# Attention block of a per-image kernel: projections split and moved, sums regrouped, four banks for the last exponent tiles, output projection in another order

## What is computed

```python
x = conv_attention(x) * gamma + x           # 32 channels, small
t = tokens(x)                               # 1024 x 256
h = layer_norm(t)
q1, k1, q2, k2, v = h@Q1.T, h@K1.T+b1, h@Q2.T, h@K2.T+b2, h@V.T     # 8 heads of 32
a1 = softmax(q1 @ k1.T / sqrt(32)); a2 = softmax(q2 @ k2.T / sqrt(32))
o = (a1 - lam * a2) @ v                     # per head
y = group_norm(o, 4 groups over all positions) @ out_w.T + out_b
t = t + y
t = t + shared_ffn(layer_norm(t)) + top2_of_8_experts(layer_norm(t))
```

## Time and profile before

| | us |
|---|---|
| median of 3 runs | 6351.29 (6344.42 to 6355.15) |
| the profiled execution's own time | 6343.51 |
| its span, first to last instruction | 6341.7 |
| TensorE busy in it | 5935.0 (94%) |
| VectorE busy | 4638.3 (73%) |
| ScalarE busy | 3218.9 (51%) |
| GpSimd busy | 3091.0 (49%) |

### The profile page before, as it was taken

One profiled execution on the slowest core, in us unless ns is written; L12 is line 12 of the kernel. 1 busy time (PEld: TensorE's weight loads), 2 busy tenths in 40 slices (PEclk: granted clock), 3 DMA queues, 4 the chain that ended last, 5 costly groups with the idle time before them and its releaser, 6 DMA issues.

```text
span 6341.7 us, 127068 instructions
## 1 busy us (share of the span) xinstructions
PE 5935.0 (94%) x41264; PEld 3784.5 (60%) x41264; DVE 4638.3 (73%) x6519; ACT 3218.9 (51%) x5724; POOL 3091.0 (49%) x1382
## 2 busy tenths in 40 slices
PE   6999999999999999999999999999999999999999
PEld 4565565655656556565565756656565565655656
DVE  5767777677776777767777677777777767677776
ACT  4545545455554545535455354554545545455454
POOL 3716537175370744707447073471735617256272
PEclk9999999999999999999999999999999999999999
DMA  2212222222222222222122221222212222121221
GB/s 74 56 49 54 58 51 51 59 49 56 53 46 59 54 55 50 46 58 55 54 52 45 62 54 53 51 48 57 55 51 53 47 60 56 46 57 44 65 56 44
DMA packets 148338, 339.05 MB, mean 53 GB/s; under 512 B 38224, under 2 KB 60880, under 8 KB 139216
## 3 DMA queue, kind: packets, MB, share of 16 engines
q1 hardware_dynamic: 147664, 330.38, 21.4%
HBM read 90.49 MB, written 17.30 MB: 17 GB/s over the span
## 4 chain that ended last, share of the span: by engine, by line
PE 70%; DVE 14%; issue 7%; ACT 4%; DMA 3%; SPq 1%; DVEq 0%; ACTq 0%
PE psum L997 16%; PE psum L1214 13%; PE psum L1145 12%; PE psum L1166 11%; DVE minus_max L742 6%; PE psum L1273 6%; PE psum L1173 4%; DVE recip_sum L763 2%; PE psum L1242 2%; DVE stage L737 2%; DMA stack<-stage 2%; PE psum L1193 1%; PE psum L1046 1%; ACT probs L497 1%; PE psum L1151 1%
## 5 line engine op out<-in xcount | busy, mean ns | idle before, releaser
L354 POOL TENSOR_TENSOR prob_sums<-probs 128x1024 f32<-128x1024 f32 x752 | 1794.4, 2386 | 3055.0 <-ACT probs L497 2629.8
L497 ACT ACTIVATE probs<-psum 128x512 f32<-128x512 f32 x4096 | 2222.6, 595 | 1428.0 <-PE psum L1214 1417.6
L742 DVE TENSOR_REDUCE minus_max<-psum 128x1 f32<-128x1024 f32 x2048 | 2417.6, 1207 | 415.7 <-PE psum L1145 410.8
L1214 PE MATMUL psum<-stack 98*128 98x512 f32 x4096 | 1451.3, 432 | 43.4 <-ACT probs L497 43.4
L1145 PE MATMUL psum<-stack 96*128 96x512 f32 x4096 | 1261.0, 414 | 129.8 <-DVE stage L737 70.7
L354 POOL TENSOR_TENSOR prob_sums<-prob_sums,probs 128x1024 f32<-128x1024 f32 x512 | 1220.2, 2383 | 72.1 <-ACT probs L497 35.7
L1166 PE MATMUL psum<-probs,v_tokens 128*32 128x256 f32 x16384 | 1111.8, 388 | 0.0
L1214 PEld LDWEIGHTS psum<-stack 98*128 98x128 f32 x4096 | 713.6, 191 | 581.0 <-ACT probs L497 447.4
L1145 PEld LDWEIGHTS psum<-stack 96*128 96x128 f32 x4096 | 725.3, 192 | 472.7 <-DVE minus_max L742 129.1
L997 PE MATMUL psum<-act_hi,w_hi 128*128 128x512 f32 x1730 | 702.3, 406 | 45.3 <-issue 26.7
L1166 PEld LDWEIGHTS psum<-probs,v_tokens 128*32 128x32 f32 x16384 | 429.0, 109 | 474.6 <-issue 297.9
(11 more groups left out here) (154 smaller groups left out, 4618.9 us busy)
## 6 DMA issues: line engine op xcount, KB each, us to landing
stack<-stage SPq DMA_DIRECT2D x1024, 128.0 KB, 3.1
stack<-stage SPq DMA_DIRECT2D x256, 256.0 KB, 3.0
prob_sums<-combine_rows_dram SPq DMA_DIRECT2D x128, 256.0 KB, 3.8
stage<-combine_rows_dram SPq DMA_DIRECT2D x128, 256.0 KB, 4.1
x_tile<-x_dram SPq DMA_DIRECT2D x17, 1024.0 KB, 4.8
x_tile<-o_head SPq DMA_DIRECT2D x512, 32.0 KB, 1.9
stack<-max_rows SPq DMA_DIRECT2D x512, 4.0 KB
y_dram<-residual SPq DMA_DIRECT2D x16, 512.0 KB, 4.5
```

The source lines that it names most:

```text
L354: nc.gpsimd.tensor_tensor(total, first, probs[:, k % NP, :], ALU.add).then_inc(sum_pool, 1)
L497: nc.scalar.activation(probs[:, k % NP, half * HALF:(half + 1) * HALF], ps[:, 4 + half, :], ACT.Exp).then_inc(p_ready, 1)
L742: v.tensor_reduce(nm[:, u % 2, q:q + 1], flat_in, AX.X, ALU.max, negate=True).then_inc(ring_free, 1)
L1214: mm(ps[:, 4 + half, :], stack[0:KS, s, 1, kt * P:(kt + 1) * P], stack[0:KS, s, 0, half * HALF:(half + 1) * HALF], start=True, stop=True). ...
```

## The change

Item order and helpers: Key projection 2 of the head of the image (`proj` 3) becomes two half items that stand among the scores of unit 0; the values tiles move with them; a part item of the units 5 to 7 stands between the two scores of its pair, with the second score behind the odd exponent tile; ScalarE takes it before the odd tile's exponential, and every whole projection is taken in two halves of 512. The stacks are loaded in the order 0, 2, 1, the `hi` pieces as soon as ScalarE has written them. Both late groups of a unit are summed in pair 0 of the next. The reciprocals stand ahead of score 2 and behind score 5, `head_out` behind score 7, `head_statistics` two tiles later.

```diff
 def ones_after(u, pair):
-    late = {2: (u, 0), 0: (u - 1, 1), 1: (u - 1, 2)}.get(pair)
-    return [late] if late and late[0] >= 0 else []
+    late = {2: ((u, 0),), 0: ((u - 1, 1), (u - 1, 2))}.get(pair, ())
+    return [(v, g) for v, g in late if v >= 0]
...
-    before = [("proj", t) for t in range(4)] + [("score", 0, q) for q in range(NT)] + [("turn", 0)]
+    before = [("proj", 0), ("proj", 1), ("proj", 2), ("score", 0, 0), ("score", 0, 1), ("part", 3, 0, 0), ("score", 0, 2),
+              ("part", 3, 1, 0)]
+    before += [("score", 0, q) for q in range(3, NT)] + [("turn", 0)]
...
+            if (u, pair) in PROJ_BESIDE:
+                items.insert(1, ("part", *divmod(PROJ_BESIDE.index((u, pair)), 2), 1))
...
+VALUES_BEHIND = {("proj", 2): (0, 1, 2), ("score", 0, 0): (3,), ("score", 0, 3): (4,), ("score", 0, 4): (5,),
+                 ("score", 0, 5): (6,), ("score", 0, 6): (7,)}
...
+TAIL = UNITS * NT - AHEAD
+LAST_EVEN = (len(RING) - 1) // 2 * 2
+def exp_bank(k):
+    return 2 if k >= TAIL and k % 2 else 4
...
-RECIP_AT, HEAD_AT = (4, 5), 6
+RECIP_AT, HEAD_AT = (2, 5), 7
...
+                    if u < 2:
+                        last = [RING_AT["proj", t] if ("proj", t) in RING_AT else RING_AT["part", t, 1, 0] for t in range(4)]
+                        sp.wait_ge(proj_hi, b * PROJ_STEPS + 4 * m + 2)
+                        sp.dma_start(*q_parts[1]).then_inc(stack_in[s], 16)
+                        sp.wait_ge(ring_free, b * len(RING) + last[2 * m] + 1)
+                        sp.dma_start(*q_parts[0]).then_inc(stack_in[s], 16)
+                        sp.wait_ge(proj_hi, b * PROJ_STEPS + 4 * m + 4)
+                        for dst, src in k_parts[:2]:
+                            sp.dma_start(dst, src).then_inc(stack_in[s], 16)
+                        sp.wait_ge(ring_free, b * len(RING) + last[2 * m + 1] + 1)
+                        sp.dma_start(*k_parts[2]).then_inc(stack_in[s], 16)
+                        return
...
-                for u in range(NST):
+                for u in (0, 2, 1):
                     load_stack(u)
...
+                for t in range(3):
+                    project(t)
+                copy_values(0)
+                copy_values(1)
+                act.wait_ge(y_out[1], b * 16 + 16)
+                for half in range(NH):
+                    project_part(3, half, 0)
+                copy_values(2)
+                copy_values(3)
...
-                        for item in BESIDE.get(divmod(k // 2 - 1, PAIRS), []) if kt % 2 == 0 else []:
+                        for item in BESIDE[u, kt // 2] if kt % 2 else []:
...
-                                                 ps[:, 4 + half, :], ACT.Exp).then_inc(p_ready, 1)
+                                                 ps[:, exp_bank(k) + half, :], ACT.Exp).then_inc(p_ready, 1)
...
+                def ahead_of_score(u, kt):
+                    if u and kt == RECIP_AT[0]:
+                        sum_recips(u - 1, 0)
...
-                norm_low(0, 1)
                 for s in range(2):
                     dve.wait_ge(o_in[s], (b + 1) * (HEADS // 2) * 4 * 16)
                 for half in range(NH):
                     cols = slice(half * HALF, (half + 1) * HALF)
                     v.tensor_scalar(on_sb[:, 1, cols], ocm[:, 1, cols], small[:, 107:108],
                                     small[:, 109:110], ALU.mult, ALU.add).then_inc(on_ready, 1)
+                    if half == 0:
+                        norm_low(0, 1)
...
                             for half in range(NH):
-                                if k >= 1:
+                                if k == TAIL + 1:
+                                    pe.wait_ge(ring_free, b * len(RING) + LAST_EVEN + 1)
+                                elif k > TAIL:
+                                    pe.wait_ge(p_ready, b * 2 * UNITS * NT + 2 * k + half - 3)
+                                elif k >= 1:
                                     pe.wait_ge(p_ready, b * 2 * UNITS * NT + 2 * k + half - 1)
-                                mm(ps[:, 4 + half, :], stack[0:KS, s, 1, kt * P:(kt + 1) * P],
+                                mm(ps[:, exp_bank(k) + half, :], stack[0:KS, s, 1, kt * P:(kt + 1) * P],
...
-                            if kt % 2 == 0:
-                                for item in BESIDE[u, pair]:
-                                    if item[0] == "score":
-                                        ring_step(item)
+                            for item in BESIDE[u, pair][slice(0, 2) if kt % 2 == 0 else slice(2, None)]:
+                                if item[0] != "turn":
+                                    ring_step(item)
...
+                def project_out(kt, half, low):
+                    pe.wait_ge(on_lo if low else on_hi, b * NH * CT + NH * kt + half + 1)
+                    cols = slice(half * HALF, (half + 1) * HALF)
+                    for k in (2 * half, 2 * half + 1):
+                        w = W_O + kt * C + (k % 2) * P
+                        for n, (wt, xx) in enumerate(((wh, xl),) if low else ((wh, xh), (wl, xh))):
+                            last = mm(ps[:, k, :], wt[:, w:w + P], xx[:, kt, cols],
+                                      start=(kt == 0 and not low and n == 0), stop=(kt == CT - 1 and low))
+                        if kt == CT - 1 and low:
+                            last.then_inc(y1_full, 1)
+                for half in range(NH):
+                    project_out(0, half, False)
                 norm_groups(1)
...
+                for half in range(NH):
+                    project_out(0, half, True)
+                for half in range(NH):
+                    project_out(1, half, False)
+                    project_out(1, half, True)
                 layer_norm()
```

More of the change, by code:

```diff
@@ L96, in ring_order @@
         for pair in range(PAIRS):
-            beside[u, pair] = []
-            for kt in (2 * pair, 2 * pair + 1):
-                n = u * NT + kt + AHEAD
-                if n < UNITS * NT:
-                    beside[u, pair].append(("score", *divmod(n, NT)))
+            items = [("score", *divmod(n, NT)) for n in (u * NT + 2 * pair + AHEAD, u * NT + 2 * pair + 1 + AHEAD)
+                     if n < UNITS * NT]
+            if (u, pair) in PROJ_BESIDE:
+                items.insert(1, ("part", *divmod(PROJ_BESIDE.index((u, pair)), 2), 1))
             if pair == TURN_AT and u + 1 < UNITS:
-                beside[u, pair].append(("turn", u + 1))
-            if (u, pair) in PROJ_BESIDE:
-                beside[u, pair].append(("part", *divmod(PROJ_BESIDE.index((u, pair)), 2)))
+                items.append(("turn", u + 1))
+            beside[u, pair] = items
     return before, beside
+VALUES_BEHIND = {("proj", 2): (0, 1, 2), ("score", 0, 0): (3,), ("score", 0, 3): (4,), ("score", 0, 4): (5,),
+                 ("score", 0, 5): (6,), ("score", 0, 6): (7,)}
 BEFORE, BESIDE = ring_order()
@@ L728, in ring_step @@
                     if item[0] in ("proj", "part"):
[L730 to L739 removed]
+                        t = item[1]
+                        pieces = [(half, half, 0) for half in range(NH)] if item[0] == "proj" else [(item[2], 0, item[3])]
+                        for half, at, g in pieces:
+                            cols = slice(half * HALF, (half + 1) * HALF)
+                            dve.wait_ge(proj_hi, b * PROJ_STEPS + 8 * g + 2 * t + half + 1)
+                            dst, hi = stage[:, 1, t, cols].bitcast(F32R), stage[:, 0, t, cols]
+                            bias = vec((V_K1B, V_K2B)[t // 2] + g)
+                            last = v.scalar_tensor_tensor(dst, wide(n % 2)[:, at, :], SCALE if t % 2 == 0 else bias, hi,
+                                                          ALU.mult if t % 2 == 0 else ALU.add, ALU.subtract)
+                        last.then_inc(ring_free, 1)
                     elif item[0] == "score":
@@ L842, in _ @@
                         kt = 2 * pair
-                        for item in BESIDE.get((u, pair), []):
+                        for item in BESIDE[u, pair]:
+                            if item[0] == "score":
+                                ahead_of_score(u, kt)
                             ring_step(item)
@@ L1136, in ring_step @@
                     elif item[0] == "part":
-                        _, t, half = item
-                        last = split_mm(slot[:, 0, :], W_QK + t * CT * C + P, (C, P), slice(half * HALF, (half + 1) * HALF))
+                        _, t, half, g = item
+                        last = split_mm(slot[:, 0, :], W_QK + t * CT * C + g * P, (C, P),
+                                        slice(half * HALF, (half + 1) * HALF))
                     elif item[0] == "score":
@@ L1200, in _ @@
                     ring_step(item)
-                    if item[0] == "score" and item[1] == 0:
-                        values(item[2])
+                    for tt in VALUES_BEHIND.get(item, ()):
+                        values(tt)
                 pe.wait_ge(v_ready, b * 4 + 4)
```

(2 more changed lines are left out.)

77 lines of the change are left out of this document (25 added, 52 removed).

## The result

| | before | after |
|---|---|---|
| time, median | 6344.8 us (6336.9 to 6355.2, 6 runs) | 6316.9 us (6310.5 to 6322.2, 6 runs) |
| ratio | | 0.9957, 95% interval 0.9947 to 0.9967 |
| profiled execution: own time | 6343.5 us | 6318.6 us |
| its span | 6341.7 us | 6316.6 us |
| its mean granted clock | 0.981 | 0.977 |

The change saves 28 us by the medians and 24.9 by the profiled executions; the forecast was 24 us. So the total came out, but it is made of terms of up to 6 us per image with both signs. The next table has the same stages in both traces, as means over the 16 images (between the starts or ends of the instructions named), with the forecast terms beside them.

A forecast was written before the change was run, and what follows sets the result against it. TensorE bounds the middle, with waits in four other places and VectorE bounding the head. Terms 2.7 - 4.6 + 1.4 - 2.1 + 1.1 = -1.5 us per image, 24 us in all: forecast 6327, own range 6305 to 6345, wider 6272 to 6372.

The forecast's parts named there:

- parts: Units 5 to 7: stalls for the part's slot go, 55.6 us against 60.2, -4.6 per image.
- sums: Units without parts: a second sum adds 0.44 in pair 0, a 0.31 stall goes; +1.4 us per image.
- a sign of being wrong: End of an image: the last L881 moving by less than half a microsecond against tile 116.
- Head: Start of an image: earlier first score, but two bubbles around the K2 halves among eight maxima; +2.7 us per image.
- What stays: Units 5 to 7: remaining costs of 8 x 0.1 turnarounds, 2 x 0.36 at turns, and 0.4 for regrouped sums.
- Last twelve tiles: End of unit work: four banks remove GpSimd's 1.42 idle, reciprocals come earlier; -2.1 us per image.
- Output projection: Image's tail: middle between ends at full and half clock for the new product order; +1.1 us per image.
- the upper end: Output projection: broken-up work stays throttled, products step at 0.43 throughout; +2.5 us per image.
- 1: Head without bubbles, or sums that cost nothing: 6262 us with both, 6295 with half of either; chance 0.22.
- 2: Pair 1 of 14 units: the first reciprocal is late and delays the maxima; slower, 6372 to 6417 us; chance 0.13.
- 3: Head: pauses around the K2 halves drop the clock, head costs 5.1; no change, about 6351 us; chance 0.11.
- 4: Last twelve tiles: four banks do nothing, GpSimd or the norm's chain takes all; 6343 us; chance 0.09.

The follow-up runs named there:

- Experiment 3: Changed kernel with K2 again a whole projection ahead of unit 0's scores and one values tile behind each score; split copies and DMA order stay: 6269.4 us.
- experiment 1: Changed kernel with the sums by ones, reciprocals, product and head statistics back where they were before: 6262.4 us.
- experiment 2: Changed kernel with the sums back in pairs 0 and 1, first reciprocal ahead of score 4, product behind score 7, head statistics two tiles later: 6220.1 us.
- Experiment 5: Changed kernel with the last twelve exponent tiles in two banks again: 6357.4 us.
- experiment 6: Changed kernel with TensorE, not GpSimd, summing tiles 3, 4 and 5 of unit 15: 6316.9 us.
- experiment 7: Changed kernel with the sum of tiles 3, 4 and 5 of unit 15 left out on both engines, so less work is done: 6312.3 us.
- experiment 4: Changed kernel with the output projection's old order and the first channel tile's low part in front again: 6297.0 us.
- experiment 8: Changed kernel, output order kept, with 17 unused filling matmuls in the output projection's pauses: 6288.5 us.
- experiment 9: Changed kernel with sums as in experiment 2, head as in Experiment 3, output order as in experiment 4; parts and four banks stay: 6151.1 us.
- experiment 10: As experiment 9, plus ten unused filling matmuls in the head, between the first four scores of unit 1: 6125.5 us.
- experiment 11: As experiment 10, but with the changed output order and the filling matmuls of experiment 8: 6109.1 us.

## Why the prediction was right, and where its terms were off

The total was right for the reasons given, by five terms of the right sign. Two sizes were off, parts by -1.3 and sums by +0.9, and they cancelled, which was luck. So was a part of the output's fit: the forecast is made on image 8, where the output stage took 12.77 before the change, at a clock of 0.87, while its mean over the images was 13.24 already. In image 8 itself the stage came to 14.58, +1.8 and not +1.1, and its end moved by 0.41 against tile 116, less than the half microsecond that the prediction set as a sign of being wrong; over the 16 images it moved by 0.80.

**The total.** Made against the profiled execution, the sum gave 6319.5, and that execution has 6318.6. The forecast of 6327 stands 10 above the median of 6316.9, for I added 7.8 us for the place of the three runs shown. With six runs the kernel before has 6344.8, so most of that was scatter of the median.

**Head, +2.7; measured +2.85.** Its steps stand: the first score came 1.02 sooner (1.2 forecast), the first maximum 0.77 behind it (0.7), each half took 3.2 from first matmul to freed slot, and the last maximum ended 14.1 behind the first score (14.25). Experiment 3 shows the same by undoing it.

**Parts, -4.6; measured -5.9.** The stalls went. What failed is the step "What stays": one more turnaround per part, 8 x 0.1, isn't there, and the turn behind the second maximum costs 0.09 and not 0.36 in pair 1 (5.23 against 3.74 + 1.4 = 5.14). With experiment 1, where the sums are out of it, parts alone are worth 60.24 - 53.13 = 7.1, more than the bound of 6.5 for no stall. The regrouped sums cost 54.33 - 53.13 = 1.2 in these units, where the forecast had 0.4. So inside this term a saving 2.1 larger (7.1, against 6.5 - 0.8 - 0.7 = 5.0) hides sums that are 0.8 dearer.

**Sums, +1.4; measured +2.3 in the units without parts.** Both halves of the mechanism hold (experiments 1 and 2): a sum adds 0.44 in pair 0, and the stall goes. What was mis-sized is the stall. I took it from one pair 0 of 3.83 as 0.31; over the units that pair lasts between 3.73 and 3.84, and in unit 1 there is no stall (3.54). At a mean stall of 0.25 the net is 0.18 or 0.19 per unit for ten units (2 to 4 and 8 to 14), and 0.43 for unit 1: 2.3. Reading one unit as if it stood for all was the error; a mean of the group would have shown it.

**Last twelve tiles, -2.1; measured -2.2.** Reciprocals 20.42 behind the first tile (20.5 forecast), and GpSimd ahead of the last exponential, as said. Experiment 5 shows that the four banks do it. Experiments 6 and 7 show what I had not seen: TensorE is so close behind GpSimd that work moved from one to the other wins nothing.

**Output projection, +1.1; measured +1.4.** This was a middle between two ends, and both can now be seen. With the clock held the stretch takes 12.58, against 12.74 to 12.84 in the best images of the kernel before: the forecast of a gain of 0.3 at most there was near. At 1.2 GHz both of the steps named are in the trace. The norm's group matmul stands behind the rounded products and starts at 4.92, not 4.08 (0.95 forecast, 0.84 measured). And the last add ends 4.47 behind the last low part, not 2.9. In most images only a part of the stretch is at 1.2 GHz, and it takes 14.6. But the upper end isn't out of reach: in images 4 and 5, with a clock of 0.66 and 0.67, it took 15.28 and 15.29, which is the +2.5 over image 8 before. That the clock is the cause rests on experiments 4 and 8 together: undoing the order takes 1.47 off, and keeping the order but filling the pauses takes 2.08 off. The Trainium skill (TensorE: Matmul & The Clock Gate, section "What's actually happening") says that activity releases the throttle; the runs agree, 1.00 with the pauses filled against 0.77. Read as "throttled throughout", that gave +2.5 in the prediction; the rows show this in two of 16 images, and the mean is +1.4.

**The rivals.** 1 is out: the bubbles are in the trace and the sum costs its 0.44. 2 is out: pair 1 is 3.74 in every unit without parts from 1 to 14, and the reciprocal ends 0.14 ahead of the maxima (a margin of 0.05 was forecast). 3 is out as a difference: the halves of K2 go at steps of 0.23, and unit 0 lasts 15.64 against 15.70. But it names a real loss that both kernels bear, worth 2.0 per image by experiments 9 and 10. 4 is out by experiment 5.

## What to carry to other kernels

A change whose total is small can be five large ones of both signs: cost each by its stage, and undo each by itself, for here the parts and the four banks kept, the head and the output order put back and the sums rearranged (experiment 9) give 194 us against the kernel before (6344.8 to 6151.1), where all five together gave 28. Before work is moved in the order of an engine, ask what it hides behind at the old place and at the new: the same sum was free in pair 1 and cost 0.44 in pair 0, and the same projection lay in TensorE's wait for a DMA at the old place and cost two bubbles among the maxima at the new. And where TensorE works in pieces with pauses between, look at the granted clock of that stretch; matmuls into an unused bank, in pauses that are there anyway, can be worth more than a better order.

## What the runs showed of the hardware

- The clock answers late. In the output projection of image 8 after the change the products at 3473.5 and 3481.2 go at steps of 0.43, those at 3479.1, right behind a wait of 1.97, at 0.23. So at nearly the same mean clock the stretch took 13.19 in one order and 14.66 in the other, by which products the slow part hit. Over the whole span TensorE was granted 1.2 GHz for 237 us before and 287 after, of which 85 and 116 lie in the output projections and about 120 and 140 in the heads with unit 0.
- Filling matmuls pay for themselves: seventeen in the output projection took 2.1 us off it per image, and ten in the head took 2.3 us off unit 0, where no matmul was removed, and lengthened the way to the first exponent tile by 0.3 (4.46 against 4.14).
- The scatter between runs went with the clock: 0.8 us between the extremes of four runs with it held at both places (experiment 11), 12 between those of six without.
